# A graph layer's gather, sum and scatter: VectorE's sum of rows and edges cut into pieces between the masks

## What is computed

```python
h = jnp.maximum(_layernorm(x, axis=-1), 0.0)
msg = jax.nn.relu(h[src] + edge_attr)
agg = jax.ops.segment_sum(msg, dst, num_segments=x.shape[0])
z = jax.nn.relu((h + agg) @ W1 + b1)
return x + z @ W2 + b2
```

## Time and profile before

| | |
|---|---|
| median of three runs | 1508.2 us (1507.06 to 1509.61) |
| the profiled execution | 1508.06 us, of which the span of its instructions 1506.2 us |
| TensorE matmuls (PE) | busy 1464.1 us, 97% |
| GpSimd (POOL) | busy 1133.5 us, 75% |
| VectorE (DVE) | busy 1010.3 us, 67% |
| ScalarE (ACT) | busy 143.9 us, 10% |
| granted TensorE clock, mean | 0.994 |

### The profile page before, as it was taken

The page is one execution under the profiler, slowest core; times in us unless marked ns, Lnnn a source line. Parts: engine busy times, 40 slices in busy tenths (PEclk is TensorE's granted clock), DMA queues, the critical chain, the costliest instruction groups (busy, mean ns, idle before and its releaser), DMA issues.

```text
span 1506.2 us, 29191 instructions
## 1 busy us (share of the span) xinstructions
PE 1464.1 (97%) x10219; PEld 792.9 (53%) x10219; DVE 1010.3 (67%) x2296; ACT 143.9 (10%) x171; POOL 1133.5 (75%) x1139
## 2 busy tenths in 40 slices
PE   2999999999999999999999999999999999999997
PEld 1555555555555555555555555555555555555554
DVE  8866676666766666666666666666666766677544
ACT  5100000000000000000000000000000000001111
POOL 5777777777777777777777777777777777777774
PEclk9999999999999999999999999999999999999997
DMA  6132232232332222223222233232232322323231
GB/s 228 38 85 85 56 85 75 65 85 56 84 85 56 85 58 83 85 56 85 70 70 85 56 85 85 56 85 57 83 85 56 85 69 72 85 56 86 60 101 35
DMA packets 67162, 115.17 MB, mean 76 GB/s; under 512 B 29810, under 2 KB 32882, under 8 KB 67010
## 3 DMA queue, kind: packets, MB, share of 16 engines
q1 hardware_dynamic: 30130, 75.86, 15.2%
q0 software_dynamic: 36000, 36.94, 12.0%
q10 hardware_dynamic: 1008, 2.06, 0.4%
HBM read 111.43 MB, written 3.34 MB: 76 GB/s over the span
## 4 chain that ended last, share of the span: by engine, by line
PE 91%; POOL 5%; issue 2%; DVE 2%; ACT 1%; DMA 0%; POOLq 0%; DVEq 0%
PE ps_cand L957 83%; PE ps L383 7%; POOL gath L347 5%; ACT agg L608 1%; DVE row_sum L702 0%; DVE row_ssq L709 0%; ACT table_hi L602 0%; PE ps L421 0%; DVE iota_pf L666 0%; DVE xh L392 0%; PE ps L406 0%; DVE xh L718 0%; PE ps L934 0%; DMA gath<-h_table,idx_pair 0%; DVE onehot L660 0%
## 5 line engine op out<-in xcount | busy, mean ns | idle before, releaser
L347 POOL DMA_INDIRECT gath<-h_table,idx_pair x1125 | 1117.9, 994 | 349.2 <-issue 312.7
L957 PE MATMUL ps_cand<-table_hi,keyhot 128*128 128x448 f16 x3409 | 1204.4, 353 | 0.0
L957 PE MATMUL ps_cand<-table_lo,keyhot 128*128 128x448 f16 x3409 | 1203.2, 353 | 0.0
L779 DVE TENSOR_TENSOR picked<-ps_cand,cand_mask 128x448 f32<-128x448 f32 x487 | 290.7, 615 | 474.4 <-PE ps_cand L957 474.2
L957 PEld LDWEIGHTS ps_cand<-table_hi,keyhot 128*128 128x128 f16 x3409 | 334.0, 98 | 313.2 <-issue 5.8
L957 PEld LDWEIGHTS ps_cand<-table_lo,keyhot 128*128 128x128 f16 x3409 | 334.0, 98 | 300.8 <-issue 1.7
L786 DVE TENSOR_REDUCE gath<-picked 128x64 f32<-128x448 f32 x487 | 266.5, 609 | 0.0
L687 DVE TENSOR_SCALAR keyhot<-key_pair,key_iota 128x512 f16<-128x512 f16 (+2 forms) x868 | 260.7, 369 | 0.1
L389 ACT ACTIVATE msg<-xh 128x832 f32<-128x832 f32 x124 | 111.5, 899 | 1333.2 <-DVE xh L805 1333.2
L383 PEld LDWEIGHTS ps<-onehot,msg 128*64 128x64 f32 x3224 | 112.3, 139 | 46.0 <-issue 46.0
L383 PE MATMUL ps<-onehot,msg 128*64 128x20 f32 (+1 forms) x3224 | 129.7, 221 | 0.0
(11 more groups left out here) (57 smaller groups left out, 83.9 us busy)
## 6 DMA issues: line engine op xcount, KB each, us to landing
edge_pair<-edges_t SPq DMA_DIRECT2D x62, 832.0 KB, 4.4
gath<-h_table,idx_pair POOLq DMA_INDIRECT x1125, 2.4
key_pair<-key_table SPq DMA_DIRECT2D x62, 256.0 KB
h_table<-xh SPq DMA_DIRECT2D x7, 224.0 KB, 2.0
x_b<-x_cols SPq DMA_DIRECT2D x1, 1568.0 KB
out<-x_sq SPq DMA_DIRECT2D x6, 224.0 KB, 5.4
idx_pair<-src_t SPq DMA_DIRECT2D x62, 13.0 KB, 1.7
xh<-x_rows ACTq DMA_DIRECT2D x4, 224.0 KB, 5.4
```

The source lines that it names most:

```text
L347: nc.gpsimd.indirect_dma_start(out=gath[u][:, r, :], out_offset=None, in_=h_table, in_offset=bass.IndirectOffsetOnAxis(ap=idx[u][:, r:r + ...
L779: nc.vector.tensor_tensor(picked[i][:, :, :], ps_cand[buf][:, 0:D * CAND].rearrange("p (d b) -> p d b", b=CAND), mask.to_broadcast([P, D, ...
L957: last = nc.tensor.matmul(bank[:, 0:D * CAND], keyhot[u % 2][:, a, i * P:(i + 1) * P], half[:, a, :, :].rearrange("p d b -> p (d b)"), sta ...
```

## The change

`sum_edges` is split into its waits (`wait_sum`) and the addition (`sum_piece`), which can cover some of the 13 rows. In `combine(c-1)` VectorE now first does the waits of the sum of chunk c-2. Then for each tile i it runs the mask, piece i of that sum, and the reduction of tile i. The last piece signals `summed`. With 4 tiles the pieces have 3, 3, 3 and 4 rows (192, 192, 192 and 256 values in each partition), with 3 tiles 4, 4 and 5, with 2 tiles 6 and 7. `add_residual` stands behind the last reduction instead of behind the last mask. Only the sum of the last chunk stays whole.

```diff
-            def combine(t, u, between=None):
+            def combine(t, u, between=None, ready=None):
                 c = t * SLOTS + u
+                if ready is not None:
+                    wait_sum(*ready)
...
                 for i in range(pe_tiles(t, u)):
...
                                             mask.to_broadcast([P, D, CAND]), ALU.mult).then_inc(masked, 1)
-                if between is not None:
-                    add_residual(between, ps[3], layer2_done, out_ready)
-                for i in range(pe_tiles(t, u)):
+                    if ready is not None:
+                        piece = sum_piece(ready[1], i, pe_tiles(t, u))
+                        if i == pe_tiles(t, u) - 1:
+                            piece.then_inc(summed, 1)
                     dve.wait_ge(masked, pe_before(t, u, i) + 1)
                     nc.vector.tensor_reduce(gath[u][:, pool_tiles(t, u) + i, :], picked[i][:, :, :], AX_X,
                                             ALU.add).then_inc(selected, 1)
+                if between is not None:
+                    add_residual(between, ps[3], layer2_done, out_ready)
...
-            def sum_edges(t, u):
+            def wait_sum(t, u):
...
-                nc.vector.tensor_tensor(edge_sum, gath[u][:, :, :], edge[u],
-                                        ALU.add).then_inc(summed, 1)
+
+            def sum_piece(u, i, n):
+                rows = slice(i * TILES_PER_CHUNK // n, (i + 1) * TILES_PER_CHUNK // n)
+                return nc.vector.tensor_tensor(edge_sum[:, rows, :], gath[u][:, rows, :], edge[u][:, rows, :], ALU.add)
+
+            def sum_edges(t, u):
+                wait_sum(t, u)
+                sum_piece(u, 0, 1).then_inc(summed, 1)
...
-                    combine(*back(t, u, 1), between)
-                if since >= 2:
-
-                    sum_edges(*back(t, u, 2))
+                    combine(*back(t, u, 1), between, back(t, u, 2) if since >= 2 else None)
...
-            combine(TURNS - 1, SLOTS - 1)
+            combine(TURNS - 1, SLOTS - 1, None, (TURNS - 1, SLOTS - 2))
...
-            sum_edges(TURNS - 1, SLOTS - 2)
             sum_edges(TURNS - 1, SLOTS - 1)
```

## The result

| | before | with the change |
|---|---|---|
| median of 13 runs each, in turn on one chip | 1506.95 us (1505.30 to 1509.61) | 1502.63 us (1502.18 to 1505.22) |
| profiled execution, its span | 1508.06, 1506.2 us | 1502.79, 1500.9 us |

The ratio is 0.9973, interval 0.9965 to 0.9981: faster by 0.27%, more than the 0.2% that can be told from no change. The bound and the mechanism of the landing were right; the landing's size was not, and the clock's part, which the forecast put at nothing, was not nothing.

A forecast was written before the change was run, and what follows sets the result against it. TensorE bounds the loop, the landing of POOL's last gather the end. POOL's -0.55 - 1.25 = -1.8 us took the profiled 1508.06 to 1506.3; the median's 0.1 more made 1506.4 us, range 1503.2 to 1509.4.

The forecast's parts named there:

- The bound: In the loop TensorE alone, 11.66 us a chunk, so longer work on VectorE costs nothing; at the end POOL decides.
- the mechanism of the landing: At the end VectorE's last sum waits for POOL's last gather to land; all behind it moves by the same 1.8 us.
- The lock: In the loop VectorE's two-input operations hold gathers, fixing POOL's phase; it moves -3.05 us, counted to a whole gather: -0.55.
- Sum for POOL: -0.55 - 1.25 = -1.8 us: POOL's last gather: -0.55 us from the loop's phase, -1.25 from the last eight chunks; ends of -0.55 and -3.1.
- The last eight chunks: From chunk 116 on, shorter holds gain POOL 1.4 us by average, about 1.25, one gather, when followed singly.
- -0.55, +0.69 and -1.80: Possible shifts in us of POOL's loop phase, -3.05 counted to within a whole gather; -0.55 was taken.
- so I leave the clock low: Behind TensorE's pause before its first layer, grown by half a microsecond, the clock stays at 1.2 GHz: no gain.
- the rival with POOL loose: Gathers slip between holds in the loop: 1503.6 us, or 1498.6 if the pause of about 2.8 us keeps 2.4 GHz; chance 0.14.
- The base: The kernel before, taken at a median of 1508.2 us, 0.1 above the profiled execution's 1508.06.
- TensorE in the last chunks: Second-layer waits save 5.6 us, five waits of some 0.65 on add_residual cost 3.3: net 2.3 us earlier, not the bound.
- The holds did not grow over the loop: Judges the slower rival: pieces hold gathers more than the sum did, chiefly in the last eight chunks; middle 1510 us, chance 0.09.
- The late phase: Rival: POOL locks at +0.69 us and gains about as much in the last chunks, 1508.2 us, no change; chance 0.12.

The follow-up runs named there:

- e1: Kernel before with only each reduction put behind its mask and add_residual behind the last reduction, sum whole in its old place: 1507.83 us, ratio 1.0004.
- e2: Kernel before with the whole sum moved right behind the last mask, ahead of the grouped reductions: 1508.44 us, ratio 1.0011.
- e4: The change with its pieces behind the masks, but reductions and add_residual grouped behind the masks as before: 1503.50 us, ratio 0.9973 to the kernel before.
- e3: Kernel before with only the sum of chunk 122 moved ahead of combine(123): 1507.65 us, ratio 1.0001.
- e22: Kernel before with 22 idle matmuls in TensorE's pause and the stray-edge branch's code as a loop: 1504.30 us, ratio 0.9979.
- e12: Kernel before with 22 idle matmuls in TensorE's pause: 1509.82 us, ratio 1.0013.
- e6: The change with five small memsets on POOL ahead of its first gather: 1504.89 us, ratio 0.9976 to the kernel before.
- e10: The change with 30 idle matmuls in TensorE's pause: 1505.25 us, ratio 0.9986 to the kernel before.
- e13: The change with 30 idle matmuls in TensorE's pause and the layers' matmuls taken out of the stray-edge branch: 1500.35 us, ratio 0.9955 to the kernel before.
- e5: The change with add_residual ahead of the last reduction instead of behind it: 1504.72 us, ratio 0.9983 to the kernel before.
- e8: The change with one tile of the last chunk moved from POOL to TensorE: 1505.54 us, ratio 0.9984 to the kernel before.
- e14: The change with one last-chunk tile moved from POOL to TensorE and the stray-edge branch's layers taken out: 1501.98 us, ratio 0.9959 to the kernel before.
- e21: The change with one last-chunk tile moved to TensorE, 16 idle matmuls in its pause, stray-edge branch as a loop: 1499.40 us, ratio 0.9947 to the kernel before.

## Why the prediction was wrong, point by point

**The bound, right.** The loop is TensorE's alone, 11.66 us a chunk before and after; VectorE's 40 us more cost nothing. The landing decided the end in the change too.

**The lock, right in rule and in size.** Before and change differ by 5.35 - 2.30 = 3.05 us in where POOL is let go, the prediction's -3.05. The pieces and compares behind hold a little more (0.01 to 0.14 us each), so at the first gather of a chunk the shift is -0.35 where I took -0.55. The warning of the Trainium skill that `tensor_tensor` was not seen to stall such DMAs (SBUF — State Buffer, "Who interferes with whom") the traces do not bear out; the same section's rule for two SBUF inputs they do, in all four rows of the table above. By that remark e1, e2 and e4 would have left POOL's place alone.

**The first step that failed: "Sum for POOL: -0.55 - 1.25 = -1.8 us".** The last gather's end moved from 1490.42 to 1487.31, 3.1 us. I split it by distances between POOL's gathers and, for the lock, against TensorE's scatter near 280 us, all read from the timelines:

- *The last eight chunks, -1.25 predicted.* From the first gather of chunk 112 to the last one's end it took 148.98 us before (148.55 in e3, 148.61 in e22, 149.78 in e12) and 146.59 with the change (146.56, 146.57 and 146.59 in e6, e10 and e13): **-2.0 to -3.2**, and -2.4 in the profiled pair. I had followed the gathers only from chunk 116. The holds of chunks 112 to 115, which I had left with the loop, went from 1.73 to 0.48 us; those from 116 on went from 2.82 to 1.69, 1.13 us, near the 1.25. Short pieces alone don't assure it: e4, which has them, took 149.06, and e5 148.10. How single gathers fall against VectorE's instructions decides there, and that I had 1.13 of it nearly right is in part luck.
- *The lock, -0.55 predicted.* It is -0.35, and one whole gather more. In the profiled change the first gather of chunk 20 stands at -12.07 against the scatter where it stood at -10.49: 1.58, near 0.35 + 1.25. In e5, e6, e8, e10 and e13 it stands at -10.82 or -10.83, without that gather. TensorE itself was 0.98 us behind in the profiled change (its scatter at 279.89 where it was at 278.91). Of the runs with the pieces, those with the whole gather more have that scatter at 279.6 to 279.9 and those without at 278.6 to 279.1, all but e4 (278.69, with it). Counted from the span's start, the two places end nearly alike: POOL's last gather ends at 1487.31 with the change and at 1487.29, 1487.47 and 1487.76 in e6, e10 and e13. I had treated a whole gather as a choice between -0.55, +0.69 and -1.80; TensorE's start, which varies by 1.3 us between the profiled runs (278.6 to 279.9), belonged in it.

For the profiled pair the first gather of chunk 112 moved from 1341.44 to 1340.72, 0.72, and from there to the end 2.39 were won: 3.11 together. The prediction had named -3.1 as an end of the term and taken -1.8.

With this the miss adds up: 1506.4 less the measured 1502.63 is 3.8 us, of which 1.3 is the landing, 1.25 the base (below), and 1.2 what is left for the clock.

**The second step that failed: "so I leave the clock low".** The tail shrank from 14.27 to 12.01 us because the clock came back 4.45 us after TensorE's first matmul behind the pause. The pause had grown by 1.66 us, from 5.14 to 6.80, and not by the half a microsecond of the forecast, so its length does not tell when the clock returns. Nor does a short pause save it: the rival with POOL loose took 2.8 us as short enough for a high clock, and behind e14's 2.79 us it was low. As a mechanism it is not the change's doing: e1 and e3 have the short tail with the whole sum (11.98 and 12.02 us), e6 and e14 the long one with the pieces (14.24 and 14.28). Like against like, the profiled kernel before would take 1508.06 - 2.26 = 1505.8 us with the change's tail, against 1502.79: 3.0 us, the landing's, and e3's profiled run says the same (1506.02). Of the first comparison's runs of the change, 8 of 13 lie at 1502.2 to 1502.8 us, all at a mean clock of 0.997, as the profiled one; the two fastest of before lie at 1505.3 and 1505.6, 3 us above. The medians' remaining 1.3 us I put down to more runs of the change getting the clock back; that is argued and not shown, since only one run of each kernel has a trace. In e6 the two kinds stand in one kernel, 2.5 us apart (medians of 1502.63 and 1505.16). What makes the clock return sooner in one execution than in another isn't settled by these runs.

**The base.** I took 1508.2 for before from three runs. Over 13 the median is 1506.95, and the profiled run was one of the long-tailed kind. Against 1506.95 my -1.8 would have said 1505.15.

**TensorE in the last chunks, right in kind, too small in size.** The waits for ScalarE before the second layer went from seven with 6.3 us to one with 0.7, and the short waits before L406 came, five of them:

```profile
PEld ps L406 <- DVE x_sq L431: 6.0, 5, 1.2
...
PE ps L421 <- ACT xh L412: 0.7, 1, 0.7
```

(the waits from 1380 to 1507 us), and TensorE's timeline in one of those places:

```profile
1412.59 0.92 PE L406 MATMUL ps<-agg,w_sb 128*64 128x448 f32 x2
1413.89 0.97 PE L406 MATMUL ps<-agg,w_sb 128*64 128x448 f32 x2 [0.39 <-DVE x_sq L431]
```

The second step starts 1.30 us after the first where 0.92 would do: 0.4 against the 0.65 I had taken, 2.1 us in five waits and not 3.3. And the 3.4 us at low clock near 1476 are gone, which the forecast had left out. Together TensorE's last scatter before the pause starts at 1481.45 where it started at 1486.15, 4.7 us earlier and not 2.3. As said, it was not the bound; e5 removed the waits and won nothing.

**The rivals.** POOL stayed caught: each gather mean of the loop is 0.99 us still. The holds did not grow over the loop: 0.43 us in a chunk in both, some 0.02 of it now by key compares. The late phase is out by the table. All three were less likely than the forecast's mechanism, which held; the range was too narrow above all because the clock stood in it only with a rival.

## What to carry to other kernels

An engine that never waits for anything but shows single slow instructions may be locked to another engine, as POOL was here: then neither its rate nor its start matters, only where in the period the other engine's holding instruction ends, and a shift counts modulo the length of one of its own instructions. Behind such an engine predict the irregular last stretch by following it instruction by instruction, from the last regular period on. And where a pause of TensorE precedes the end of a kernel, price its work behind the pause at both clocks (14.3, 12.0 and 9.8 us here), and look for the code that a branch makes it jump over.

## What the runs showed of the hardware

- An indirect DMA of 128 rows takes POOL 0.943 us and 0.305 between two. One issued while VectorE runs a `tensor_tensor` with two SBUF inputs is held until 0.13 us before that ends, to 0.01 us in four kernels. In the trace of before all 119 gathers issued during a sum were held, and none of the 121 issued during a mask (L779), whose one input is in PSUM, 118 of them issued more than 0.03 us ahead of that moment.
- A key compare, a `tensor_scalar` on fp16 with one SBUF input, holds such a DMA too: by up to 0.10 us in the change, and by 0.46 to 0.81 us for single ones in e2, e4 and e6, across the compares that follow.
- TensorE behind a pause of 5.14 us (before) or 6.80 us (the change) ran at 1.2 GHz, and behind one of 2.79 us too (e14). It returned to 2.4 GHz 4.45 us after its first matmul in the change, and stayed at 1.2 to the end, 13 us on, in before. With idle matmuls in all but 2.3 us of the pause (e10, e13, e22) it stayed at 2.4: the 50 scatter matmuls took 1.80 us where they took 3.05.
- A never-taken branch with long code cost 2.75 to 2.9 us at the jump in e8, e10 and e12, whose instruction queue shows 15 packets, and nothing in the traces with 14. A loop in place of the unrolled code inside the branch cured it, and with a tile more on TensorE and 16 idle matmuls gave the fastest version with nothing left out, e21: 1499.40 us, 0.9947 of the kernel before.
- On one of the five further chips the same kernels took 22% longer, with hundreds of gaps in TensorE's stream; there the change's gain was gone.
